# Two programs made one: the weight preparation, the pads and the tables between a decoder layer's attention and its experts

## The reference

```
x = layernorm(x + self_attention(x))       # 16 heads of 16, one shared key and value head
x = layernorm(x + cross_attention(x, ctx)) # 120 context rows, two-layer projections, an additive mask
comb = two largest of softmax(x @ Wg.T), normalised, 8 experts
out = sum over e of ((a * sigmoid(b)) @ Wo.T + bo) * comb[e],  where a, b = split(x @ W1[e].T + b1[e])
x = layernorm(x + out)
```

## Time and profile before

| | us |
|---|---|
| median of 3 runs | 1470.23 (1467.3 to 1477.19) |
| the profiled execution | 1475.48 |
| its span, first to last instruction | 1472.9 |
| PE / DVE / ACT / POOL busy | 1276.2 / 1136.1 / 755.9 / 656.9 |
| mean granted clock of TensorE | 0.952 of full |

### The profile page before, as it was taken

How to read it: one execution, slowest core, us unless ns; L and a number is a source line. 1 busy time by engine, 2 the same in 40 slices (tenths; PEclk the granted TensorE clock), 3 DMA queues, 4 the chain that set the end, 5 groups by cost and what they waited for, 6 DMA issues and landing times. The chain is left out here.

```text
span 1472.9 us, 29966 instructions
## 1 busy us (share of the span) xinstructions
PE 1276.2 (87%) x7668; PEld 899.1 (61%) x7669; DVE 1136.1 (77%) x3110; ACT 755.9 (51%) x1743; POOL 656.9 (45%) x1018
## 2 busy tenths in 40 slices
PE   6888999999999999999987307999999999968886
PEld 4443555555555555555544206888888888858876
DVE  1455788888888888888864387888888888859998
ACT  1125677777777777777775242223223322314444
POOL 1011244454544444545444472343334333447886
PEclk9998999999999999999997558999999999989999
DMA  4436456656646656655636522334433443369995
GB/s 101 106 61 101 80 104 132 127 117 133 122 120 128 128 116 122 129 120 117 122 107 234 197 81 84 130 130 133 137 131 130 133 137 130 130 247 322 336 334 198
DMA packets 171822, 211.67 MB, mean 144 GB/s; under 512 B 20048, under 2 KB 143056, under 8 KB 167632
## 3 DMA queue, kind: packets, MB, share of 16 engines
q1 hardware_dynamic: 147808, 143.92, 40.9%
q0 software_dynamic: 17680, 55.28, 10.1%
q10 hardware_dynamic: 6240, 11.34, 2.2%
HBM read 124.81 MB, written 84.89 MB: 142 GB/s over the span
## 5 line engine op out<-in xcount | busy, mean ns | idle before, releaser
L853 DVE TENSOR_REDUCE negmax<-psS 128x2 f32<-128x512 f32 x512 | 349.2, 686 | 100.1 <-PE psS L625 94.4
L755 ACT ACTIVATE probs<-psT 128x512 f32<-128x512 f32 x512 | 303.4, 598 | 171.7 <-PE psT L635 165.1
L1331 ACT ACTIVATE sig<-hb 128x512 f32<-128x512 f32 x136 | 86.1, 633 | 286.9 <-DVE hb L1414 279.8
L625 PE MATMUL psS<-kstack,qstack 96*128 96x256 bf16 x1024 | 195.4, 273 | 33.8 <-DVE kstack L949 15.3
L635 PE MATMUL psT<-qstack,kstack 99*128 99x512 bf16 x512 | 194.9, 382 | 5.1 <-ACT probs L755 5.1
L1211 POOL DMA_INDIRECT g_rows<-g,slot x136 | 135.6, 997 | 70.7 <-issue 67.4
L625 PEld LDWEIGHTS psS<-kstack,qstack 96*128 96x128 bf16 x1024 | 92.4, 104 | 90.7 <-DVE negmax L853 34.8
L391 POOL DMA_INDIRECT lists<-x,slots x128 | 127.0, 992 | 34.2 <-issue 30.3
L523 PE MATMUL psO<-probs,vaug 128*32 128x512 f32 x1024 | 140.4, 621 | 0.9 <-ACT probs L755 0.8
L1425 DVE SCALAR_TENSOR_TENSOR g<-g,xe,sig 128x512 f32<-128x512 f32 x136 | 102.2, 751 | 28.5 <-DVE g L1421 16.8
L1414 DVE TENSOR_TENSOR hb<-psHb,f_b 128x512 f32<-128x512 f32 x136 | 94.0, 691 | 37.5 <-issue 34.7
(11 more groups left out here) (201 smaller groups left out, 2950.7 us busy)
## 6 DMA issues: line engine op xcount, KB each, us to landing
rows<-g_rows SPq DMA_DIRECT2D x32, 1024.0 KB, 8.0
qstack<-q_parts SPq DMA_DIRECT2D x192, 128.0 KB
xe<-lists SPq DMA_DIRECT2D x136, 133.0 KB, 2.1
q_parts<-qpart SPq DMA_DIRECT2D x32, 384.0 KB, 2.8
sums<-x SPq DMA_DIRECT2D x32, 264.0 KB, 2.3
x2in<-sums SPq DMA_DIRECT2D x32, 264.0 KB, 4.7
xt<-in_x_t SPq DMA_DIRECT2D x32, 256.0 KB, 6.0
xres<-in_x SPq DMA_DIRECT2D x32, 256.0 KB, 3.2
```

The lines of the kernel that those rows point to most:

```text
L625: last = mm(psS[:, u % 2, hh * S:(hh + 1) * S], qstack[0:KROWS, b1.s4, 2 * hp + hh, c * P:(c + 1) * P], kstack[0:KROWS, b1.s4, :], start=T ...
L755: nc.scalar.activation(probs[:, u % PT, :], psT[:, u % 2, :], ACT.Exp, scale=SELF_SCALE).then_inc(sm["exp_done"], 1)
L853: v.tensor_reduce(negmax[:, b1.s2, 2 * hp:2 * hp + 2, c], psS[:, u % 2, :].rearrange("p (h k) -> p h k", h=2), AX.X, ALU.max, negate=True) ...
```

## The change

The two phases keep their work and their loops, but `attention` and `experts` now return functions, and one block has for each engine one program: first its attention part, then its experts part. There is no meeting of engines between them; what was guarded by it is guarded by semaphores. SBUF is placed by hand so that buffers of both phases live together where they must; the weights' buffers are laid out expert by expert (`piece`). Besides:

- ACT rounds the weights within the drain: experts 4 and 5 at the end of step B+3, 6 at place 0 of B+4 (after the norm that stands there), 7 at place 7, 0 and 1 at place 12, 2 and 3 at places 7 and 12 of step B+5.
- DVE makes all eight splits: two at place 3 of step B+4, one at place 6, three at place 3 of B+5 (after the slots of block 30), two after the tables.
- The bias loads and the load of `wo` go from step B+1 and the experts block to SP's step B+4, behind waits for block 31's cross scores and their mask. The order of the loads of `w1_raw` stays 0 to 7.
- POOL's constants and the pads' clearing go to the end of the first `qpart` of step 0; POOL stores the pads there to a DRAM buffer `pad_rows`. After the slots, SP copies them behind the lists' ends in DRAM, eight copies with a row number read from `pad_tab`, instead of POOL's eight scatters.
- The tables are made by long operations over 128x136x8 instead of the loop over experts.
- The products get the weights' address from a function of the row block, `e * 2048 + k * 1024`, in each matmul.

```diff
+W1_ORDER = (4, 5, 6, 7, 0, 1, 2, 3)
+def split_w1(ops, eng, dram, nth):
+    part = dram["piece"](W1_ORDER[nth])
+    eng.wait_ge(dram["w1_rounded"], nth + 1)
+    ops.tensor_tensor(dram["w1_lo"][:, part], dram["w1_raw"][:, part], dram["w1_hi"][:, part].bitcast(F32), ALU.subtract
+                      ).then_inc(dram["w1_split"], 1)
...
         def load_experts(t):
-            if t.n == B + 1:
-                (bo and eight b1 loads)
             if t.n == B + 3:
                 wait(sp, "pv_done", 4 * B)
                 wait(sp, "exp_done", UNITS * B)
                 for e in range(E):
-                    sp.dma_start(dram["w1_raw"][:, :, e * H2:(e + 1) * H2],
+                    sp.dma_start(dram["w1_raw"][:, dram["piece"](e)].rearrange("p (c h) -> p c h", c=DC),
...
+            if t.n == B + 4:
+                wait(sp, "cross_scored", B)
+                wait(sp, "mask_ready", B)
+                (bo load)
+                wait(sp, "score_link", B)
+                (wo load, eight b1 loads)
...
+            if t.n == 0:
+                expert_constants()
...
+        def round_w1(e):
+            act.wait_ge(dram["w1_loaded"][e], 16)
+            if e == 4:
+                act.wait_ge(dram["pads_stored"], 32)
+            if e == 0:
+                wait(act, "cross_scored", B)
+                wait(act, "mask_ready", B)
+            copy(dram["w1_hi"][:, dram["piece"](e)], dram["w1_raw"][:, dram["piece"](e)]
+                 ).then_inc(dram["w1_rounded"], 1)
+        rounds = {(B + 3, 15): W1_ORDER[0:2], (B + 4, 0): W1_ORDER[2:3], (B + 4, 7): W1_ORDER[3:4],
+                  (B + 4, 12): W1_ORDER[4:6], (B + 5, 7): W1_ORDER[6:7], (B + 5, 12): W1_ORDER[7:8]}
...
+        splits = {(B + 4, 3): 2, (B + 4, 6): 1, (B + 5, 3): 3}
...
+    def sync(sp, drained):
+        sp.wait_ge(dram["pads_stored"], 32)
+        sp.wait_ge(sm["pads_placed"], 1)
+        for e in range(E):
+            row = sp.value_load(pad_tab[0:1, e:e + 1], min_val=0, max_val=(E - 1) * STRIDE + T)
+            sp.dma_start(dram["lists"][bass.ds(row, P), :], dram["pad_rows"][e * P:(e + 1) * P, :]
+                         ).then_inc(sm["pads_written"], 16)
+        drained(sp)
         sp.wait_ge(sm["tables_ready"], 2)
-        sp.wait_ge(sm["pads_written"], 16 * (E + 1))
+        sp.wait_ge(sm["pads_written"], 16 * E)
...
-        for e in range(E):
-            link(v.tensor_scalar(past[:, :], number[:, :], upto[:, e:e + 1], None, ALU.is_ge))
-            link(v.scalar_tensor_tensor(rowf[:, :], past[:, :], skip[:, e:e + 1], rowf[:, :], ALU.mult, ALU.add))
-            link(v.tensor_tensor(expf[:, :], expf[:, :], past[:, :], ALU.add))
+        link(v.tensor_tensor(below[:, :, :], upper[:, :, :], ntile[:, :].unsqueeze(1).to_broadcast([P, E, E]), ALU.mult))
+        v.tensor_scalar(skip[:, :], ntile[:, :], -float(P), float(STRIDE), ALU.mult, ALU.add)
+        link(v.tensor_reduce(upto[:, :], below[:, :, :], AX.X, ALU.add))
+        link(v.tensor_tensor(past[:, :, :], number[:, :].unsqueeze(2).to_broadcast([P, TILES, E]),
+                             upto[:, :].unsqueeze(1).to_broadcast([P, TILES, E]), ALU.is_ge))
+        link(v.tensor_tensor(past_skip[:, :, :], past[:, :, :], skip[:, :].unsqueeze(1).to_broadcast([P, TILES, E]),
+                             ALU.mult))
+        link(v.tensor_reduce(rowf[:, :], past_skip[:, :, :], AX.X, ALU.add))
+        link(v.scalar_tensor_tensor(rowf[:, :], number[:, :], float(P), rowf[:, :], ALU.mult, ALU.add))
...
+        link(v.tensor_reduce(expf[:, :], past[:, :, :], AX.X, ALU.add))
...
+        for nth in range(halved, E):
+            split_w1(v, dve, dram, nth)
...
+        def expert(w, e, first):
+            return lambda k: w[:, bass.ds(e * (DC * H2) + (k * H2 + first), H)]
```

More of the change, by code:

```diff
@@ L193, in attention @@
     slots = sb("slots", [P, 2, QC * 2], U32)
-    base = dram["base"]
     psS = ps("psS", [P, 2, 512])
@@ L432, in _, with tensor @@
         pipeline(pool, step)
[L433 to L438, removed]
+    def tensor(pe):
         mm = nc.tensor.matmul
@@ L963, in step @@
                     last.then_inc(sm["y2_ready"], 1)
+                for _ in range(splits.get((t.n, u), 0)):
+                    split_w1(v, dve, dram, halved)
+                    halved += 1
             if t.fixed and t.n == 0:
@@ L1035, in experts @@
     exp_tab = sb("exp_tab", [P, TILES], I32)
[L1036 to L1041, removed]
+    pad_tab = sb("pad_tab", [P, E], I32)
     xe = sb("xe", [P, 4, ROW])
     hb = sb("hb", [P, 2, H])
-    g = sb("g", [P, 4, H])
     sig = sb("sig", [P, 2, H])
@@ L1171, in _, with gpsimd @@
         pair_pipeline(sp, pair_step)
[L1173 to L1198, removed]
+    def gpsimd(pool):
         def step(t):
@@ L1493, in decoder_layer @@
             "stride": stride,
             "out": out,
[L1495 to L1501 removed]
+            "semaphores": ctx,
+            "w1_piece": D // P * H2,
+            "piece": lambda e: slice(e * (D // P) * H2, (e + 1) * (D // P) * H2),
+        }
+        DC, H, QC, W1 = D // P, H2 // 2, 2, E * (D // P) * H2
@@ new lines, in decoder_layer, with place @@
+        dram["w1_loaded"] = [ctx.enter_context(nc.semaphore(f"w1_loaded{e}")) for e in range(E)]
+        with ExitStack() as late:
+            def place(name, shape, dt=F32):
+                dram[name] = late.enter_context(nc.sbuf_tensor(name, shape, dt))
+            place("b1", [P, E * H2])
+            place("bo", [P, D])
+            with nc.sbuf_tensor("result", [P, 4, QC, D], F32) as result:
+                dram["result"] = result
+            place("w1_hi", [P, W1], F32R)
+            with nc.sbuf_tensor("w1_raw", [P, W1], F32) as w1_raw:
+                dram["w1_raw"] = w1_raw
+            with (nc.sbuf_tensor("rows", [P, 4, QC, 2 * H], F32) as rows, nc.sbuf_tensor("row_sum", [P, 4, H], F32) as row_sum,
+                  nc.sbuf_tensor("x2in", [P, 4, QC, D + E], F32) as x2in, nc.sbuf_tensor("y", [P, 4, QC, D], F32) as y):
+                dram.update(rows=rows, row_sum=row_sum, x2in=x2in, y=y)
+            place("w1_lo", [P, W1], F32R)
+            second = experts(nc, late, io, dram)
@@ new lines, in decoder_layer, with _ @@
+        with ExitStack() as early:
+            first = attention(nc, early, io, dram)
+        block = ctx.enter_context(nc.Block())
+        @block.sync
+        def _(sp):
+            first["sync"](sp)
+            second["sync"](sp, first["drained"])
+        @block.gpsimd
+        def _(pool):
+            first["gpsimd"](pool)
+            second["gpsimd"](pool)
+        @block.tensor
+        def _(pe):
+            first["tensor"](pe)
+            second["tensor"](pe)
+        @block.scalar
@@ L1505, with _ @@
+        def _(act):
+            first["scalar"](act)
+            second["scalar"](act)
+        @block.vector
+        def _(dve):
+            halved = first["vector"](dve)
+            second["vector"](dve, halved)
 def kernel(**inputs):
```

220 lines of the change are left out of this document (102 added, 118 removed).

## The result

Over four runs each the changed kernel took 1452.4 us in the median (1449.0 to 1452.5), the kernel before 1471.6 us (1467.3 to 1477.2): a ratio of 0.9862, with a 95% interval of 0.9825 to 0.9899. That is 19 us less, where 26 were forecast. The profiled execution took 1452.3 us, its span was 1449.7.

What follows compares the result with a forecast made beforehand. The seam between the phases was taken to decide: pads' constants, tables, splits. Starting PE 37.8 us earlier, less 11.5 us of drain slip (7.6+0.6+3.3), gives 26.3 us less and a median of 1444 us, range 1432 to 1456.

Steps and rivals of the forecast that it cites:

- rival A: Whole kernel: the forecast itself holds, 1444 us; chance 0.58.
- rival C: Drain and pads: larger slip or late pads, 6 to 10 us more, 1450 to 1454 us; chance 0.13.
- ACT, step B+3: Drain: roundings of experts 4 and 5 before block 31's first norm wait for expert 5's load; norm 7.6 us later.
- ACT, step B+4: Drain: rounding 6 between block 31's norm and the x1t copy costs 0.6 us, bounds 0.6 and 1.0.
- DVE, step B+5: Drain: three splits beside POOL's second rstd of block 31 delay its `shift` by 3.3 us, bounds 0 and 5.6.
- Tables: Seam: DVE's tables, made by long operations, end 8.0 us after the end of the last slots.
- Splits: Seam: the two DVE splits left behind the tables take 4.4 us, ending 12.4 us after the last slots.
- Pads: Seam: SP's eight pad copies, issued 1.15 us apart, land 11.9 us after the last slots; bounds 11.4 and 15.5.
- Bias loads and pads' constants at the start: Moved bias loads in SP's drain cost 0; POOL's clearing and constants after the first `qpart` cost 0, or up to 2 us.
- Rival E: Tile loop: address arithmetic in each matmul adds 0.37 us a tile, 1494 us; sign: periods above 3.04 us; chance 0.05.
- Rival B: Drain: does not slip, or by a third; 37.8 us less 0 to 4 gained, 1432 to 1436 us; chance 0.20.
- rival D: Seam and drain: gathered work costs the drain 27.8 us, leaving 10 of 37.8 us, 1460 us; chance 0.04.

Runs made afterwards that it cites:

- e1: Changed kernel with the eight raw weight loads issued in the order of their rounding (4 to 7, then 0 to 3): 1445.5 us, 0.9822 of before.
- e5: Kernel before, with all eight weight splits made by DVE and none by POOL: 1468.5 us, 0.9969 of before.
- e4: Changed kernel with no rounding or split in the drain; ACT rounds after its last gate exponentials, DVE splits after the tables: 1447.9 us.
- e8: Changed kernel with the old table loop over experts and an unused 3808-byte buffer restoring the changed kernel's tile loop addresses: 1451.1 us.
- e9: Kernel of e7 plus an unused buffer of 288 bytes per partition ahead of the tile loop's buffers: 1434.5 us, 0.9756 of before.
- e2: Changed kernel with DVE waiting for POOL's second rstd of block 31, then two splits instead of three, the third behind the tables: 1450.2 us.
- e10: Kernel of e7 plus an unused buffer of 1600 bytes per partition ahead of the tile loop's buffers: 1439.5 us.
- e3: Changed kernel with the tables made by the old loop over experts, whose smaller buffer moves the tile loop's addresses: 1452.4 us.
- e7: Changed kernel with the edits of e1 and e2 together, plus pad copies on two queues (four on SP, four on ACT): 1438.8 us, 0.9767 of before.

## Why the prediction came out as it did

The direction and the mechanism held, and the measured median lies in the range. It does not lie at rival A's 1444 us, though, but in rival C's band of 1450 to 1454. C's cause came true in part, since POOL's rstd went to nearly the far bound of 5.6 us; another part of the distance, 3.4 us in the tile loop, was in no term. The first tile was forecast 26.3 us earlier and started 26.5 us earlier. That agreement is luck: 4.1 us of it are T, and from T it is 22.4 us. By the prediction's steps:

- **ACT, step B+3**, forecast +7.6: the norm came 8.2 us later against T, because expert 5 landed at 815.2, T+11.4, where the kernel before had it at T+10.8. Right, and e1 shows it as the cause.
- **ACT, step B+4**, forecast +0.6: 1.1, since rounding 6 waited for its own load (0.47 us in ACT's row above), just over the upper bound of 1.0.
- **DVE, step B+5**, forecast +3.3 with 5.6 as the far bound: +5.4. This term was mis-sized. The working let two of four POOL operations meet a split; three did, as `nmean` began 0.02 us after the first split. In the trace `nmean` ended 0.05 us after the first split, `rstd` 0.6 us after the second, `shift` 0.05 us after the third: one operation for each split of 2.2 us. The 14.0 us of `past`, which the far bound was modelled on, have another pattern, one operation over three POOL splits of 4.5 us. The row of `past` even starts at 862.23, 0.5 us ahead of the first of them, and 0.5 us is all that it takes by itself. e5, where none of the eight `past` takes more than 0.50 us, shows that the wait goes with POOL's splits, but no run shows why it lasted for three. The three terms of the drain make 14.7 us, and S-T grew by 14.4.
- **Tables**, forecast S+8.0: S+7.5. **Splits** S+12.4: 11.9. **Pads** S+11.9: S+12.9, because the copies were issued 1.27 us apart in the median, not 1.15. The first tile came at S+16.0 instead of 15.0.
- **Bias loads and pads' constants at the start**, forecast 0: e4 has the drain of before to 0.1 us with both in place, and the start shows no loss: the first row maximum stands at 42.5 us, before at 43.3.
- **Behind the seam** nothing was forecast, and 3.4 us were lost: the tile loop took 426.6 us instead of 423.2. The period is 3.021 us against 3.005 (from 100 tiles each), 2.2 us over 136 tiles. e8 and e9 show that addresses alone move the period by more than this, 0.029 us; that they are the cause between these two kernels too is likely but not tested by itself. PE also waited once for a tile's load for 1.1 us, which it did not before. Rival E had a slower loop by address arithmetic. That is refuted: the high line has its 132 register operations of 46 ns in 100 us as in the earlier trace rows, the line behind it has 132 more of 32 ns in both kernels, and the third line none. The prediction's sign for E, a period above 3.04 us, came from the whole loop divided by 136, with its slow start in it; tile by tile the kernel before stood at 3.005:

```profile
L1249 PEldq FUSED_REGOPS  x132: 42/46/60, 1000.6 to 1098.1; - x132
```

The sum is 83.1-60.7-3.4 = 19.0 us, beside 19.2 between the medians. Against the forecast 2.9 us went into the drain, 1.0 into the pads and 3.4 into the tile loop. Rival B fell in e4 and e1; rival D had the right question, but with the wrong size: the drain's work cost 14.5 us, and its removal gave 5 back.

One sum in the prediction is wrong, without effect on the forecast: the chances of A, B and C add up to 0.91, not 0.89. And one of its signs missed by little: PE's gap ahead of the first tile was to be 15 us at most and was 17.6.

## What to carry to other kernels

Work put in front of an idle engine's next wait is free only if its own inputs are there: load in the order of use, and look up the landing of the very load that it waits for. Here ACT stood 10.88 us in front of a load, and the order of use (e1) brought the last slots 6.7 us earlier. Where a GpSimd chain is on the path, compare it with and without long VectorE operations beside it: here four operations took 6.9 us beside the splits and 1.4 us when the splits stood behind them (e2). When the hole is closed, read what ends last again (here the issue of eight small copies), and compare the pace of loops that the change did not touch.

## What the runs showed of the hardware that was not expected

- Where buffers lie in SBUF moves PE's pace at an unchanged clock: a tile takes 3.021 us in eight executions of the changed kernel and its variants, 3.017 in e10 with its 1600 bytes more, and 2.992 in e3 and e9 (1405 and 1407 matmuls in 300 us). The kernel before and e5, whose layout is another, have 3.005.
- A scatter's issue on POOL is also longer beside splits: 3.08 and 1.82 us in e2 for the first two of four, 1.04 and 0.96 in the changed kernel, whose splits have ended by then; e7 has the figures of e2. Beside the long table operations (1.29 us each) it is longer too: the second of the last four scatters took 1.96 us in the changed kernel, and 0.96 in e3 and e8 with their short table operations.
- The start of the drain scattered over 12 us between executions that share the code before it. Up to 11 us arise before 242 us and up to 6 in the last 50 us ahead of T; in between all traces agree within 1 us.
